# Attention with a mixture of experts: shared matmuls ahead of an output's first product, the normalisation over two steps, the router inside the projection, the slot table moved at other times

## The chip, the core and the metric

The kernel runs on one core of a Trainium2 chip. A core has TensorE (PE in the profile: matmuls; PEld: its weight loads), VectorE (DVE), ScalarE (ACT), GpSimd (POOL) and the DMA queues that SyncE (SP), ScalarE and GpSimd issue to. The metric is the device time of one execution in microseconds (us), as the median of several runs.

## The reference, cut to what matters

```python
x = L0_attn_x                                   # (2, 1024, 512)
xn = _layernorm(x)
x = x + _L0_attn_ref(xn, Wq, Wk, Wv, Wo) + _L0_ffn_ref(xn, router, bias, gate, up, down, shared ...)
# attention, 16 heads of 32
S = where(causal, Q K^T / sqrt(32), -1e30);  P = softmax(S);  out = (P V) @ Wo.T
# feed-forward, 2048 tokens
scores = sigmoid(x2d @ rw.T);  sfc = scores + bias            # 8 experts
# the best 2 of 4 groups of 2 experts, in them the best 2 experts, weights scaled to a sum of 2.5
routed = sum over e of cw[:, e] * ((silu(x2d @ gw[e].T) * (x2d @ uw[e].T)) @ dw[e].T)   # 352 wide
shared = (silu(x2d @ sg.T) * (x2d @ su.T)) @ sd.T                                       # 704 wide
out = routed + shared
```

## The kernel before

Each fp32 operand of the large products is split into a high and a low part, and three products stand for one (hi·hi, hi·lo, lo·hi). The program is five blocks, one after the other; a block begins when all engines have ended the one before.

1. `norm_phase`: normalises 16 tiles of 128 tokens, turns them into `xt_hi` and `xt_lo`, projects V. Its last steps split the router's weights into `r_hi` and `r_lo`.
2. `project_phase`: first the router, then Q and K. TensorE makes the router's logits for four blocks of 512 tokens (12 matmuls each into the one buffer `ps_r`, which ScalarE copies out in between), turns them, ScalarE takes the sigmoid, and GpSimd picks the experts. Then `multiply` makes 8 chunks of 128 rows of Q and K, four groups of 12 matmuls each; for each chunk ScalarE and VectorE split the weights (`split`, L524 and L654), and the results go out in two parts (`evacuate`). SP loads the weights of a chunk (L476), stores `xt` blocks and stores each chunk when it is evacuated, in one written order of steps.
3. `attend_phase`: 32 heads (16 for each of 2 batches) of 12 steps. Every engine runs the same loop over steps `s`, and a table of lags says what of which head it does in a step: at lag 0 the row maxima of scores (`maximum`, TensorE L1392 into one of two `ps_m`, VectorE L1272 or L1276 out of them), at lag 14 the maxima turned (`turn_row`, L1403) and sent through DRAM into a row of `qs` by ScalarE's queue (L1186, L1194), at 24 the scores (L1416), then exponential, the split into `prob_hi` and `prob_lo` (GpSimd L1160 in 10 of 12 steps, VectorE L1291 in 2), and at 30 the product with V (`value`, L1439 and L1441). A head has two outputs, one for each half of its queries; both build up in the one buffer `ps_o`. The first product of an output (`n in STARTS`) waits until ScalarE has copied the output before it (`o_copied`, L1218, in the same step's list). At lag 32 the copied output is turned into `ps_x`, and at 33 VectorE normalises it (`normalize`: L1307, L1308, L1310, L1315), before it takes that step's maximum. `turn_row` writes into the same bank `ps_x`, and so waits for `o_ready`, the end of L1315.
   In `shared(s)` TensorE puts 864 matmuls of the shared expert between the steps. A planner (`fill_counts`) deals them out by what each step costs TensorE. In the steps with the first product of an output it puts one to three.
   GpSimd makes the slot table of the routed tokens in between (`place`): it fills the table with pads, SP stores it to DRAM (L989, at `g == 1`), 32 indirect DMAs scatter the entries over it (L1130), and after the last step GpSimd reads it back (L1171) and waits for it.
4. `out_phase`: the attention's last product. 5. `routed_phase`: 39 tiles of gathered tokens.

## Time and profile before

| what | value |
|---|---|
| median of 3 runs | 1184.96 us (1183.19 to 1187.52) |
| profiled execution, its own time | 1182.23 us |
| its span | 1180.5 us |
| PE busy | 1064.8 us (90%), 5379 matmuls |
| DVE busy | 780.8 us (66%) |
| ACT busy | 647.6 us (55%) |
| POOL busy | 508.1 us (43%) |
| DMA moved | 165.70 MB, mean 140 GB/s |

The span is what the engines' records cover; the profiled execution's own time is 1.7 us longer. A matmul's recorded end is modelled, and matmuls overlap in the array: in an undisturbed run a matmul of 512 columns is recorded at 0.39 us while the next starts 0.23 us after it.
### The profile page before, as it was taken

Reading aid. Unit: us, or ns where it says so; the run is one execution under the profiler, and the core shown is the slowest. Engines: PE = TensorE matmul, PEld = TensorE weight load, DVE = VectorE, ACT = ScalarE, POOL = GpSimd, SP = SyncE. Lnnn points to the kernel's source line nnn. Section 1 sums busy time; section 2 is a strip of 40 time slices with the busy share of each in tenths; the row PEclk is TensorE's granted clock in tenths of the full one; section 3 lists DMA queues with packets and bytes.
Section 4 is the critical chain, followed back from the end, with each engine's and each line's share of the span. In section 5 each row is a group of like instructions: output and inputs, shape, how many; then the busy total and the mean of one; then the engine's idle time right before and its main releaser. Section 6 shows DMA issues by size and latency. Waiting matters only on the chain. (4 is left out here: it accounts for less than half of the span.)

```text
span 1180.5 us, 19294 instructions
## 1 busy us (share of the span) xinstructions
PE 1064.8 (90%) x5379; PEld 816.7 (69%) x5380; DVE 780.8 (66%) x1729; ACT 647.6 (55%) x1291; POOL 508.1 (43%) x567
## 2 busy tenths in 40 slices
PE   6979995888999999989999999978988999999994
PEld 4838883666677776767777777756766777777773
DVE  6822324556678868777777787645466777778772
ACT  4532220455777767777777777752154555555551
POOL 0008305289656555556556555651002333333331
PEclk9999995889899999999999999998989999999998
DMA  6969549978255264344345535018895443333342
GB/s 206 311 267 371 205 193 198 142 117 144 44 144 144 50 193 109 121 124 127 94 116 144 144 78 183 2 37 276 259 342 140 72 71 63 68 70 69 71 72 36
DMA packets 104648, 165.70 MB, mean 140 GB/s; under 512 B 49040, under 2 KB 59600, under 8 KB 101360
## 3 DMA queue, kind: packets, MB, share of 16 engines
q1 hardware_dynamic: 94128, 143.88, 42.8%
q0 software_dynamic: 9856, 20.53, 9.8%
q8 instruction: 38, 0.62, 0.2%
q14 instruction: 50, 0.41, 0.1%
q10 hardware_dynamic: 576, 0.26, 0.1%
HBM read 103.35 MB, written 61.28 MB: 139 GB/s over the span
## 5 line engine op out<-in xcount | busy, mean ns | idle before, releaser
L1160 POOL TENSOR_TENSOR prob_lo<-prob,prob_hi 128x512 fp32r<-128x512 f32 (+2 forms) x320 | 308.8, 978 | 239.6 <-ACT prob_hi L1209 223.9
L1202 ACT ACTIVATE prob<-ps_s 128x512 f32<-128x512 f32 (+3 forms) x384 | 188.2, 490 | 150.2 <-PE ps_s L1421 104.0
L1209 ACT ACTIVATE prob_hi<-prob 128x512 fp32r<-128x512 f32 (+3 forms) x384 | 198.5, 517 | 12.8 <-ACT row_stage L1183 12.7
L1272 DVE CUSTOM_DVE_ANT_0 ps_m<-ps_m,causal 128x384 f32<-128x384 f32 (+3 forms) x256 | 126.0, 498 | 69.8 <-PE ps_m L1392 68.9
L1828 DVE TENSOR_TENSOR rw_lo<-gu_sb,rw_hi 128x704 fp32r<-128x704 f32 x156 | 138.8, 893 | 47.9 <-ACT rw_hi L1763 42.2
L1742 POOL DMA_INDIRECT out<-work,rows x39 | 61.7, 1582 | 243.4 <-DVE rows L1789 118.0
L1392 PE MATMUL ps_m<-ks,qs 96*128 96x512 f32 (+3 forms) x384 | 143.7, 376 | 22.6 <-DMA ks<-qk_hi 13.6
L1439 PE MATMUL ps_o<-prob_hi,vs 128*66 128x512 f32 (+3 forms) x384 | 133.9, 349 | 18.8 <-issue 11.5
L1763 ACT ACTIVATE rw_hi<-gu_sb 128x704 fp32r x156 | 123.3, 792 | 46.6 <-PE ps_ru L1861 31.6
L1416 PE MATMUL ps_s<-qs,ks 97*128 97x512 f32 (+3 forms) x384 | 138.7, 361 | 2.4 <-ACT prob L1202 2.3
L1441 PE MATMUL ps_o<-prob_lo,vs 128*66 128x512 f32 (+3 forms) x384 | 131.1, 342 | 0.0
L1276 DVE TENSOR_REDUCE maxima<-ps_m 128x1 f32<-128x512 f32 x128 | 85.5, 685 | 65.7 <-PE ps_m L1392 65.4
L1392 PEld LDWEIGHTS ps_m<-ks,qs 96*128 96x128 f32 x384 | 75.4, 197 | 54.9 <-DVE maxima L1276 23.8
L1882 PE MATMUL ps_ry<-d_sb,work 128*128 (+1 forms) x234 | 106.9, 592 | 1.2 <-issue 1.2
L1416 PEld LDWEIGHTS ps_s<-qs,ks 97*128 97x128 f32 x384 | 74.2, 193 | 20.4 <-ACT prob L1202 4.7
L1439 PEld LDWEIGHTS ps_o<-prob_hi,vs 128*66 128x66 f32 x384 | 53.7, 140 | 43.5 <-issue 22.5
L1472 PE MATMUL ps_f<-xt,sg_hi 128*128 128x512 f32 (+1 forms) x192 | 74.7, 424 | 8.0 <-DVE gated L1325 4.3
L1754 ACT ACTIVATE xg_hi<-ps_xt 128x512 fp32r<-128x512 f32 x39 | 23.3, 598 | 85.9 <-PE ps_xt L1849 85.9
L1472 PE MATMUL ps_f<-xt,su_hi 128*128 128x512 f32 (+1 forms) x192 | 70.4, 400 | 0.0
L1882 PEld LDWEIGHTS ps_ry<-d_sb,work 128*128 128x128 f32 (+1 forms) x234 | 43.2, 190 | 38.8 <-issue 38.8
L662 DVE TENSOR_TENSOR work<-ps_q,work 128x512 fp32r<-128x512 f32 x32 | 22.2, 692 | 61.1 <-ACT work L531 61.1
L1421 PE MATMUL ps_s<-late,eye 128*128 128x128 f32 x256 | 61.2, 239 | 0.0
(212 smaller groups left out, 2422.4 us busy)
## 6 DMA issues: line engine op xcount, KB each, us to landing
xt<-xt_blocks SPq DMA_DIRECT2D x8, 2048.0 KB, 9.2
v_rows<-work SPq DMA_DIRECT2D x16, 512.0 KB, 2.9
qk_hi<-work SPq DMA_DIRECT2D x8, 1024.0 KB, 4.5
qk_lo<-work SPq DMA_DIRECT2D x8, 1024.0 KB, 7.1
qs<-qk_hi SPq DMA_DIRECT2D x64, 128.0 KB, 2.9
ks<-qk_hi SPq DMA_DIRECT2D x64, 128.0 KB, 3.1
vs<-v_rows SPq DMA_DIRECT2D x32, 256.0 KB, 4.8
out<-y_acc SPq DMA_DIRECT2D x32, 256.0 KB, 3.5
```

Source lines behind the costliest of these rows:

```text
L1160: nc.gpsimd.tensor_tensor(prob_lo[:, s % NPL, 0:w], prob[:, s % NP, 0:w], prob_hi[:, s % NPH, 0:w].bitcast(F32), ALU.subtract).then_inc(lo ...
L1202: nc.scalar.activation(prob[:, s % NP, 0:w], ps_s[s % NS][:, 0:w], ACT.Exp, scale=SCALE).then_inc(exp_done, 1)
L1209: nc.scalar.activation(prob_hi[:, s % NPH, 0:w], prob[:, s % NP, 0:w], ACT.Copy).then_inc(hi_ready, 1)
L1272: nc.vector.tensor_tensor_reduce(ps_m[s % NM][:, 0:w], ps_m[s % NM][:, 0:w], causal[:, TBW - w:], 1.0, MASKED, ALU.add, ALU.max, maxima[:, ...
L1392: nc.tensor.matmul(ps_m[s % NM][:, 0:w], qs[0:ROWS, c, t * P:(t + 1) * P], ks[0:ROWS, c, k0:k0 + w], start=True, stop=True).then_inc(m_don ...
L1416: last = nc.tensor.matmul(ps_s[s % NS][:, 0:w], ks[0:ROWS + 1, c, kt * P:(kt + 1) * P], qs[0:ROWS + 1, c, q0:q0 + w], start=True, stop=not ...
L1439: nc.tensor.matmul(into, vs[:, c, kt, :], prob_hi[:, s % NPH, 0:w], start=n in STARTS, stop=False)
L1441: nc.tensor.matmul(into, vs[:, c, kt, :], prob_lo[:, s % NPL, 0:w], start=False, stop=n in ENDS).then_inc(pv_done, 1)
L1472: last = nc.tensor.matmul(ps_f[part][0:w, :], (w_hi, w_lo, w_hi)[term][:, kc, f0:f0 + w], xt[:, (0, 0, 1)[term], kc, :], start=(j == 0), s ...
L1763: nc.scalar.activation(w_hi[:, k, :], chunk(e, k), ACT.Copy).then_inc(w_hi_ready, 1)
L1828: nc.vector.tensor_tensor(w_lo[:, k, :], chunk(e, k), w_hi[:, k, :].bitcast(F32), ALU.subtract).then_inc(w_lo_ready, 1)
L1882: last = nc.tensor.matmul(ps_y[c % 2][:, :], hid_t[0:w, c % HR, k, :], d_sb[0:w, bass.ds(e * NF + k, 1), :].rearrange("p a d -> p (a d)"), ...
```

## The change

- **TensorE in attention.** In a step with an output's first product, `shared(s)` now comes before `value`; in all others it stays behind it.
- **VectorE in attention.** `normalize` keeps the reciprocal and the copy; the sum and the multiplication become `weigh_o`, one step later and behind that step's maximum. Three semaphores become one.
- **Projection.** The router's four groups of 12 matmuls now each follow a group of the first chunk, and the turn follows the first group of the second chunk. The sigmoid comes after ScalarE's second copy of that chunk. The chunks' weights are converted first. ScalarE's wait for the stores of the norm block moves in front of its first copy-out.
- **Slot table.** Its pads are written by GpSimd at the start of the projection and stored by SP in step 5 of its list there, behind the load of chunk 5. The table is read back by SP in front of `load_values(15)`, at `g == 16`, and SP waits for it at the block's end.
- Some semaphores are merged, and ScalarE's loop over the chunks is unrolled.

```diff
@@ project_phase, SP
+                def store_pads(i, c):
+                    if i == 2 and c == 1:
+                        sp.wait_ge(table_padded, 3)
+                        sp.dma_start(slots_dram.rearrange("(j p) a -> p j a", p=P),
+                                     slot_table[:, :, :]).then_inc(pads_stored, 16)
-                pipeline(sp, CH, U, [(0, load), (0, store_xt), (1, load_shared), (2, store)],
+                pipeline(sp, CH, U, [(0, load), (0, store_xt), (1, load_shared), (0, store_pads), (2, store)],
                          back=CH)
+                sp.wait_ge(pads_stored, 16)
@@ ACT
+                        if t == 0:
+                            copy_logits(n)
+                        if t == 1 and n == 1:
+                            act.wait_ge(logits_turned, 1)
+                            nc.scalar.activation(score[:, :, :], ps_s[:, :, :],
+                                                 ACT.Sigmoid).then_inc(score_ready, 1)
-                pipeline(act, CH, U, [(0, split), (1, evacuate)])
+                pipeline(act, CH, U, [(0, split), (1, evacuate)], back=CH)
@@ PE
                         last.then_inc(q_done, 1)
+                        if t == 0:
+                            logits(n)
+                        if t == 1 and n == 0:
+                            turn_logits()
@@ attend_phase, SP
-                    if g == 1:
-                        sp.wait_ge(table_padded, 1)
-                        sp.dma_start(slots_dram.rearrange("(j p) a -> p j a", p=P),
-                                     slot_table[:, :, :]).then_inc(pads_stored, 16)
+                    if g == HEADS // 2:
+                        sp.wait_ge(entries_stored, 16 * 2 * NT)
+                        sp.dma_start(slot_table[:, :, :],
+                                     slots_dram.rearrange("(j p) a -> p j a", p=P)
+                                     ).then_inc(table_loaded, 16)
@@ GpSimd
-                pool.wait_ge(entries_stored, 16 * 2 * NT)
-                pool.dma_start(slot_table[:, :, :], slots_dram.rearrange("(j p) a -> p j a", p=P)
-                               ).then_inc(table_loaded, 16)
-                pool.wait_ge(table_loaded, 16)
@@ DVE
                     nc.vector.reciprocal(o_inv[:, :, :], ps_ot[:, :, 2 * DK:2 * DK + 1]).then_inc(normalizing, 1)
                     nc.vector.tensor_copy(o_part[:, :, :], ps_ot[:, :, DK:2 * DK]).then_inc(normalizing, 1)
+                def weigh_o(s):
...
+                    dve.wait_ge(normalizing, 3 * o + 2)
                     nc.vector.tensor_tensor(o_sum[:, :, :], ps_ot[:, :, 0:DK], o_part[:, :, :],
+                                            ALU.add).then_inc(normalizing, 1)
+                    dve.wait_ge(normalizing, 3 * o + 3)
...
-                    for lag, stage in ((NORM, normalize), (0, maximum), (LO, lo)):
+                    for lag, stage in ((NORM, normalize), (0, maximum), (LO, lo),
+                                       (NORM + 1, weigh_o)):
@@ PE
-                    for lag, stage in ((AHEAD, score), (VALUE, value)):
-                        if 0 <= s - lag < STEPS:
-                            stage(s - lag)
-                    shared(s)
+                    if 0 <= s - AHEAD < STEPS:
+                        score(s - AHEAD)
+                    starts = (s - VALUE) % NB in STARTS
+                    if starts:
+                        shared(s)
+                    if 0 <= s - VALUE < STEPS:
+                        value(s - VALUE)
+                    if not starts:
+                        shared(s)
```

TensorE in attention, from the maximum in front of a head's last block of the second output to the maximum of the next step. `ps_m` holds maxima, `ps_s` scores, `ps_o` the output, `ps_f` the shared expert. Before:

```order
L1392 MATMUL ps_m<-ks,qs 128x384
L1416 MATMUL ps_s<-qs,ks 128x512
L1439 MATMUL ps_o<-prob_hi,vs 66x512
L1441 MATMUL ps_o<-prob_lo,vs 66x512
L1497 MATMUL ps_f<-sd_lo,hid_hi 128x512
L1392 MATMUL ps_m<-ks,qs 128x512
```

The same place of TensorE's order now:

```order
L1409 MATMUL ps_m<-ks,qs 128x384
L1433 MATMUL ps_s<-qs,ks 128x512
L1514 MATMUL ps_f<-sd_lo,hid_hi 128x512
L1456 MATMUL ps_o<-prob_hi,vs 66x512
L1458 MATMUL ps_o<-prob_lo,vs 66x512
L1409 MATMUL ps_m<-ks,qs 128x512
```

One matmul of the shared expert (L1497, now L1514) has moved from behind the two products to between the score and the first product.

VectorE in attention, over the first two steps of a head, from the last maximum of the head before. Before:

```order
L1280 TENSOR_TENSOR maxima<-maxima 128x4
L1307 RECIPROCAL o_inv<-ps_x 128x4
L1308 COPY o_part<-ps_x 128x128
L1310 TENSOR_TENSOR o_sum<-ps_x,o_part 128x128
L1315 TENSOR_TENSOR work<-o_sum,o_inv 128x4x32
L1276 TENSOR_REDUCE maxima<-ps_m 128x1
L1352 TENSOR_TENSOR y_acc<-ps_f,y_acc 128x512
L1276 TENSOR_REDUCE maxima<-ps_m 128x1
```

VectorE's same place now:

```order
L1291 TENSOR_TENSOR maxima<-maxima 128x4
L1316 RECIPROCAL o_inv<-ps_x 128x4
L1317 COPY o_part<-ps_x 128x128
L1287 TENSOR_REDUCE maxima<-ps_m 128x1
L1368 TENSOR_TENSOR y_acc<-ps_f,y_acc 128x512
L1287 TENSOR_REDUCE maxima<-ps_m 128x1
L1327 TENSOR_TENSOR o_sum<-ps_x,o_part 128x128
L1331 TENSOR_TENSOR work<-o_sum,o_inv 128x4x32
```

The sum and the multiplication have moved behind two reductions (and, in this head, a sum of the shared expert); the first reduction now stands right behind the copy.

SP's queue in attention at `g == 16`, now:

```order
L960 DMA ks<-qk_hi 32x1024
L1010 DMA slot_table<-slots 128x39x2
L967 DMA vs<-v_rows 128x8x64
L998 DMA gu_raw<-in_sgate 128x4x96
L998 DMA gu_raw<-in_sup 128x4x96
```

The table's read stands between the rows of head 16 and the values of head 15; before, GpSimd issued it after its last step.

## Rows read from the trace of the kernel before

**Rows 1.** Busy time by stretch: span, us (x instructions) of each engine, PEclk, DMA, GB/s.
```profile
69.40:88.40 19.00, 14.47 (x64) 5.33 (x64) 0.72 (x2) 4.94 (x8) 1.61 (x4) 0.91 0.72 272
88.40:176.90 88.50, 88.42 (x416) 72.88 (x416) 27.78 (x46) 21.68 (x38) 35.76 (x62) 1.00 0.68 256
...
305.00:755.00 450.00, 430.09 (x2361) 330.37 (x2360) 352.81 (x909) 334.83 (x758) 253.03 (x264) 1.00 0.42 119
```

**Rows 2.** Timeline of the projection's start: start us, us, engine, line, [idle before <-releaser].
```profile
69.49 0.43 PE L543 MATMUL ps_r<-xt_hi,r_hi 128*8 128x512 f32 x1 [2.52 <-PEq L228]
...
69.83 0.46 SPq L476 DMA_DIRECT2D w_raw<-in_wqk  x1
...
87.03 1.14 ACT L524 ACTIVATE w_hi<-w_raw 128x512 fp32r<-128x512 f32 x2
...
88.42 0.50 PE L563 MATMUL ps_q<-xt_hi,w_hi 128*128 128x512 f32 x1 [1.68 <-DVE w_lo L654]
```

**Rows 3.** Landing of the eight loads of the chunks' weights (`w_raw`).
```profile
DMA to landing us min/median/max: 3.2/7.0/8.1
```

**Rows 4.** A stretch while the pads are stored, columns as in rows 1.
```profile
200.00:204.00 4.00, 4.00 (x14) 3.11 (x13) 1.46 (x3) 0.00 (x0) 0.04 (x1) 0.65 2.08 2
```

**Rows 5.** DMA issues: queue, count, KB each, median us to landing.
```profile
slots<-slot_table SPq DMA_DIRECT2D x1, 39.0 KB, 27.6
slot_table<-slots POOLq DMA_DIRECT2D x1, 39.0 KB, 6.6
```

**Rows 6.** Timeline of attention's first head, behind the pads' store.
```profile
216.44 0.60 ACT L1226 ACTIVATE tanh<-ps_f 128x512 f32<-128x512 f32 x1 [6.67 <-DMA max_rows<-row_stage]
...
217.81 0.74 PE L1472 MATMUL ps_f<-xt,sg_hi 128*96 128x512 f32 x1 [4.31 <-DVE gated L1325]
...
221.87 0.79 PE L1416 MATMUL ps_s<-qs,ks 97*128 97x512 f32 x1
```

**Rows 7.** An output's first product: timeline, and its group from 305 to 755 us.
```profile
561.88 0.39 PE L1416 MATMUL ps_s<-qs,ks 97*128 97x512 f32 x1
562.45 0.41 PE L1439 MATMUL ps_o<-prob_hi,vs 128*66 128x512 f32 x1 [0.18 <-issue]
...
L1439 PE MATMUL ps_o<-prob_hi,vs 128*66 128x512 f32 (+3 forms) x317 | 109.3, 345 | 10.9 <-issue 6.3 <-ACT o_copy L1218 4.6
```

**Rows 8.** Normalisation and maxima: timeline, group (305 to 755 us), lines' minimum/median/maximum ns.
```profile
572.15 0.29 DVE L1310 TENSOR_TENSOR o_sum<-ps_x,o_part 128x128 f32<-128x128 f32 x1
572.49 0.40 PE L1392 MATMUL ps_m<-ks,qs 96*128 96x512 f32 x1
572.55 0.84 DVE L1315 TENSOR_TENSOR work<-o_sum,o_inv 128x128 f32<-128x128 f32 x1
573.32 0.68 DVE L1276 TENSOR_REDUCE maxima<-ps_m 128x1 f32<-128x512 f32 x1
574.05 0.44 PE L1392 MATMUL ps_m<-ks,qs 96*128 96x384 f32 x1 [0.23 <-DVE maxima L1276]
574.33 0.27 PE L1403 MATMUL ps_x<-ident,maxima 128*8 128x128 f32 x1
...
L1392 PE MATMUL ps_m<-ks,qs 96*128 96x512 f32 (+3 forms) x316 | 114.0, 361 | 6.0 <-DVE maxima L1276 5.0
...
L1315 DVE TENSOR_TENSOR work<-o_sum,o_inv x64: 292/712/1921, 241.4 to 791.3; 128x128 f32<-128x128 f32 x64
...
L1280 DVE TENSOR_TENSOR maxima<-maxima x32: 164/910/1101, 198.5 to 754.6; 128x4 f32<-128x4 f32 x32
```

**Rows 9.** Timeline of attention's end.
```profile
788.56 2.10 POOL L1171 DMA_DIRECT2D slot_table<-slots  x1
...
798.37 0.34 DVE L1603 COPY rows<-slot_table 128x1 int32<-128x1 int32 x4 [6.76 <-PEq L923]
```

**Rows 10.** ScalarE's queue in a middle head: the row of maxima stored, then loaded.
```profile
471.37 0.27 ACTq L1186 DMA_DIRECT2D max_rows<-row_stage  x1
477.98 0.22 ACTq L1194 DMA_DIRECT2D qs<-max_rows  x1
```

More of the change, by code:

```diff
@@ L429, in project_phase @@
         bias_b = sbuf("bias_b", [P, 1, E])
+        pads = sbuf("pads", [P, 1], I32)
         score = sbuf("score", [P, NT, E])
@@ L501, in store_xt, with copy_logits @@
                                      ).then_inc(xt_stored, 16)
-                pipeline(sp, CH, U, [(0, load), (0, store_xt), (1, load_shared), (2, store)],
+                pipeline(sp, CH, U, [(0, load), (0, store_xt), (1, load_shared), (0, store_pads), (2, store)],
                          back=CH)
                 sp.wait_ge(xt_stored, 32 * NTB)
+                sp.wait_ge(pads_stored, 16)
             @block.scalar
             def _(act):
-                act.wait_ge(zeros_stored, 32)
-                for slot_stored in norm_stored:
-                    act.wait_ge(slot_stored, 16 * (NT // NORM_SLOTS))
-                for n in range(NTB):
+                def copy_logits(n):
                     act.wait_ge(logits_done, n + 1)
@@ L516, in _ @@
                                          ACT.Copy).then_inc(logits_copied, 1)
-                act.wait_ge(logits_turned, 1)
-                nc.scalar.activation(score[:, :, :], ps_s[:, :, :], ACT.Sigmoid).then_inc(score_ready, 1)
                 def split(i, c):
@@ L527, in evacuate @@
                     t = U * i + c
+                    if t == 0:
+                        act.wait_ge(zeros_stored, 32)
+                        for slot_stored in norm_stored:
+                            act.wait_ge(slot_stored, 16 * (NT // NORM_SLOTS))
                     wait(act, stored[c], 32 * i)
@@ L532, in evacuate, with logits @@
                                              ACT.Copy).then_inc(q_hi_ready, 1)
-                pipeline(act, CH, U, [(0, split), (1, evacuate)])
+                        if t == 0:
[5 more added lines that the diff above has]
+                pipeline(act, CH, U, [(0, split), (1, evacuate)], back=CH)
             @block.tensor
             def _(pe):
-                for n in range(NTB):
-                    pe.wait_ge(logits_copied, n) if n else None
+                def logits(n):
+                    wait(pe, logits_copied, n)
                     j = 0
@@ L547, in _, with turn_logits @@
                     last.then_inc(logits_done, 1)
-                pe.wait_ge(logits_copied, NTB)
-                for t in range(NT):
-                    last = nc.tensor.transpose(ps_s[:, t, :], logits_t[:, t * P:(t + 1) * P],
-                                               ident[0:E, 0:E])
-                last.then_inc(logits_turned, 1)
+                def turn_logits():
+                    pe.wait_ge(logits_copied, NTB)
+                    for t in range(NT):
+                        last = nc.tensor.transpose(ps_s[:, t, :], logits_t[:, t * P:(t + 1) * P],
+                                                   ident[0:E, 0:E])
+                    last.then_inc(logits_turned, 1)
                 def multiply(i, c):
@@ L588, in _ @@
             def _(pool):
+                nc.gpsimd.iota(pads[:, :], pattern=[[0, 1]], base=T, channel_multiplier=1
+                               ).then_inc(table_padded, 1)
+                nc.gpsimd.memset(slot_table[:, :, 1], 0.0).then_inc(table_padded, 1)
+                pool.wait_ge(table_padded, 2)
+                nc.gpsimd.tensor_copy(slot_table[:, :, 0].bitcast(I32),
+                                      pads[:, :].broadcast_to([P, NST])).then_inc(table_padded, 1)
                 nc.gpsimd.memset(ones[:, :], 1.0).then_inc(ones_ready, 1)
@@ L658, in evacuate @@
                     t = U * i + c
+                    if t == U - 1:
+                        dve.wait_ge(logits_turned, 1)
                     for n in range(NTB):
@@ L847, in attend_phase @@
         tile_no = sbuf("tile_no", [P, NST, 1])
-        pads = sbuf("pads", [P, 1], I32)
         tokens = sbuf("tokens", [P, NT], I32)
@@ L1033, in place @@
                 def place():
-                    then(nc.gpsimd.iota(pads[:, :], pattern=[[0, 1]], base=T, channel_multiplier=1))
-                    then(nc.gpsimd.memset(slot_table[:, :, 1], 0.0))
-                    yield
-                    placed()
-                    nc.gpsimd.tensor_copy(slot_table[:, :, 0].bitcast(I32),
-                                          pads[:, :].broadcast_to([P, NST])).then_inc(table_padded, 1)
-                    yield
                     then(nc.gpsimd.iota(tokens[:, :], pattern=[[P, NT]], base=0,
@@ L1298, in normalize @@
                     half = BLOCKS[s % NB][0]
-                    g = s // NB
-                    h, b = g // B, g % B
-                    o = 2 * g + half
+                    o = 2 * (s // NB) + half
                     dve.wait_ge(o_turned, o + 1)
```

65 lines of the change are left out of this document (31 added, 34 removed).

## The prediction

> **What bounds the kernel now.** I read three views. The busy time by stretch comes first [rows 1]: in the projection TensorE is busy 88.42 of 88.50 us at full clock, and in the body of attention 430 of 450 us, while no other engine comes near. So in both a term counts only if it shortens what TensorE does or waits for. Then the timelines at the seams of the blocks: the projection begins with router work in which TensorE is busy 14.47 of 19.00 us [rows 1, 2], attention's first head stands on a row of maxima [rows 6], and its end on GpSimd's table read [rows 9]. Last the groups and timelines inside a head, for the two places at which TensorE waits in the body: an output's first product [rows 7] and the third maximum of a head [rows 8]. The page's engine shares alone would have hidden both, since matmuls overlap in the record: between starts at 561.88 and 562.45 lie 0.57 us where 0.23 would do, so 0.34 are lost, of which the record calls 0.18 idle [rows 7].
>
> **Part 1, shared matmuls in front.** A stretch of 27 heads has 54 first products. The group's idle time is 10.9 us [rows 7]; if each also hides the 0.16 us by which an end is recorded late (0.34 less 0.18), the loss is at most 10.9 + 54 x 0.16 = 19.5 us, 0.20 to 0.36 us for each. What is put in front costs 0.23 us each, and it is work that TensorE does anyway, one to three of them, so most of such a wait is covered. Over 64 outputs the waits are 13 to 23 us. I take 15 saved. The far ends: 20 saved; and 3 lost, if the covered waits are replaced (a moved matmul waits for its own input, or a product that did not wait comes one or two matmuls later and ScalarE's chain after it).
>
> **Part 2, the normalisation over two steps.** What goes: in the head shown, the third maximum starts at 574.05 after 0.23 us recorded idle plus the 0.16, so 0.39 lost, because the reduction that frees its buffer starts only at 573.32, behind the multiplication [rows 8]. The group's idle, 6.0 us over 27 heads, plus 0.16 for each, is the same 0.38. Now that reduction comes right behind the copy, and the wait goes. What comes: turning the maxima waits for the multiplication's end. That now stands behind the second maximum (start 572.49) and its reduction: 0.40 for the matmul, 0.68 for the reduction, 0.29 for the sum, 0.11 up to the multiplication (572.15 + 0.29 to 572.55) and 0.71 for itself, the line's median: 2.19 us after 572.49. TensorE's own work reaches the turn 574.33 - 572.49 - 0.39 = 1.45 us after it. So it waits 0.74, less the 0.39 gone: 0.35 us a head, and a little more for the semaphores between. Behind the waiting turn on TensorE stand the next scores and products, so all of it counts: 31 heads x 0.39 = 12 us more. The ends: at the line's shortest, 0.29, it comes to 31 x (0.35 - 0.42) = -2 us; at 1.10, the longest of a similar instruction (L1280), 31 x (0.35 + 0.39) = +23. The second output's normalisation is in a step where nothing waits for it: nothing.
>
> How long the multiplication takes is the disputed number: 292 ns at best, 712 in the median [rows 8], for the same shape. The Trainium skill has a rule for it (SBUF — State Buffer, "Who interferes with whom"): a VectorE instruction with two SBUF inputs and a GpSimd instruction that reads SBUF exclude each other for a whole instruction. L1310, which has one input in PSUM, takes 0.29 in the same head, and L1315, with both in SBUF, 0.84: the rows agree. By that rule the multiplication goes on waiting wherever GpSimd is at work, and the term stays near +12; without it, it would be near -2.
>
> **Part 3, the pads' store leaves attention.** Around it DMA stands: from 200 to 204 us 2 GB/s are moved at a share of 2.08 [rows 4], and the store of 39 KB lands after 27.6 us [rows 5]. ScalarE cannot load the row of maxima and stands 6.67 us, so `gated` is late, and TensorE stands 4.31 us until 217.81 [rows 6]. Its matmuls behind that pause are recorded at 0.74 and 0.79 us instead of 0.39 [rows 6], so the 221.87 - 217.81 = 4.1 us to the first score would be about 2. So 4.3 + 2 = 6.3, and the rest of the slow stretch and the late rows of the next head, which I put at 1.7: 8 us saved (5 to 11). What is late next is the row itself, in its normal 6.6 us [rows 10], which five steps cover.
>
> **Part 4, the table's read leaves the end.** GpSimd issues it at 788.56 and it lands 6.6 us later [rows 5, 9]; VectorE stands 6.76 us until 798.37, so it had ended at 791.61. Without the read the next block follows VectorE's end by the seam alone. At the projection's start TensorE's whole pause, seam and all that it waited for, was 2.52 us [rows 2], so the seam is between nothing and that: the block begins at 791.6 to 794.1, which is 6.8 to 4.3 us earlier. I take 5.5.
>
> **Part 5, the read in the middle.** The same 39 KB, now in pieces through SP's queue beside head 16's rows. Nothing of it is needed there; what it can delay is the row of maxima, stored at 471.37 and loaded at 477.98 [rows 10], with about five steps of room in front and four behind it. A step is 450 / 324 = 1.39 us, so the room is 12.5 us. If the read takes 6.6 us it is hidden; if it takes the pads' 27.6, ScalarE stands and TensorE with it, up to 27.6 - 12.5 = 15 us. The nearer row is the read's own, 6.6, so I take +1.5. The Trainium skill speaks against a gain from the change of queue (DMA: Bandwidth & Descriptors, "Issuing engines are not separate DMA queues"): all issuers share the same 16 engines, and the rows of ScalarE's queue interleave with SP's. No run here shows this for a read of the table.
>
> **Part 6, the projection.** No matmul goes. The router work, 14.47 us with its slow-clock part (the stretch's mean clock is 0.91 [rows 1]), no longer waits for ScalarE's copies, but TensorE now begins only when the first weights are there: issued at 69.83, landed 3.2 to 8.1 us later [rows 2, 3], 4 if nothing is in front of it, and then 88.42 - 87.03 = 1.39 for both conversions: 75.2. Plus 14.47 it is 89.7 where the chunks' work stood alone at 88.42: 1.3 us later, and the pause before is longer, so more of it may be at half clock. I take +1.5 (0 to 5). The sigmoid, and with it GpSimd's routing, comes 17 to 20 us later; GpSimd is busy 35.76 of the 88.50 us, so it has that room. The pads' store is hidden if the weights behind it come in time: chunk 6's are issued a chunk (88.5 / 8 = 11 us) after it and used two chunks later (about 21). At worst 27.6 - 11 + 8.1 - 21 = 3.7 us late. In the median nothing.
>
> **The sum.** -15 + 12 - 8 - 5.5 + 1.5 + 1.5 = -13.5 us, against the profiled execution's 1182.2: 1168.7. That execution was 2.7 us under the median 1184.96; on the median it is 1171.5, and I say 1172.
>
> **Rivals.**
> A, the multiplication finds GpSimd idle. Where it stands now, a step later, GpSimd waits for ScalarE more often; then part 2 is -2 and the sum -27.5: 1157.5. For it: the range down to 292 ns; GpSimd is busy only 253 of 450 us [rows 1]. Against: the median.
> B, the transfers' cost moves instead of going. The pads delay the projection's weights (+3.7), and the table's read costs ScalarE and TensorE 8 in the middle, half of its far end: -13.5 + 3.7 + 6.5 = -3.3: 1181.7. Against it: DMA's mean share in the body is 0.42 [rows 1].
> C, the order of the shared matmuls gives nothing, since ScalarE's chain sets when the next scores and products can go: -13.5 + 15 = +1.5: 1186.5. Against it: ScalarE is busy 335 of 450 us.
> D, slower: the turn of the maxima takes more than all the rest gives. Without part 2 the sum is -25.5, so it is slower from (25.5 + 3.6) / 31 = 0.94 us a head, with a multiplication of 0.94 - 0.39 + 0.71 = 1.26 us. If each took the 1.92 of the line's longest, a head would lose 0.39 + 1.21 = 1.60, in all 49.6: +24, 1209. In heads with a sum of the shared expert between the two reductions 0.68 comes on top. Against: L1280, caught in the same way, is at most 1.10.
>
> **How the numbers follow.** A measurement of this kernel tells a change from none at about 0.3%, 3.6 us. Forecast 0.50, A 0.18, B 0.09, C 0.11, D 0.12 (its milder cases mostly, 1189 to 1200). Faster: 0.48 of the forecast's 0.50 + 0.18 of A + 0.04 of B, and 0.02 of C = 0.72. Within: 0.02 + 0.05 + 0.07 = 0.14. Slower: 0.12 of D and 0.02 of C = 0.14. The likeliest case alone, from its own ends: 1162 to 1181. The range, to leave out 2 in 10: 1156 to 1187.
>
> **What would show it.** First products: the group's idle time of PE falls from 10.9 to under 3 us in the same stretch. Part 2: L1392 no longer waits for VectorE, and the turn of the maxima starts late behind the second half of the normalisation, by some 0.7 us; if that line's median is near 0.3, A holds. Part 3: ScalarE's wait of 6.67 us for `max_rows` and TensorE's of 4.31 are gone, and the first score comes at full clock. Part 4: out_phase begins within 3 us of VectorE's last instruction. Part 5: ScalarE shows no wait for `max_rows` near head 16. Part 6: the projection's last matmul ends 0 to 3 us later than 176.9. The forecast is wrong if the body of attention does not get shorter by 2 to 5 us, or if the seams together give under 8.

## The result and the profile after

The changed kernel takes 1166.35 us (median of 4 runs, 1161.82 to 1170.92), the kernel before beside it 1184.08: a ratio of 0.985, 95% interval 0.980 to 0.989. It is faster, as forecast, by 17.7 us where about 13 were forecast (1172 against a median of 1184.96). The profiled execution took 1170.92, span 1169.1, and is the slowest of the four; against the 1182.23 of the profiled execution of before the difference is only 11.3 (13.5 forecast). One of the six executions of e9 below ran in a slower state (1216.45 us at a granted clock of 0.83), so the time given there is the median of the other five (over all six it is 1154.11).

Busy time by stretch of the changed kernel, to hold against [rows 1]; the columns are those of the view there:

```profile
69.40:88.40 19.00, 11.94 (x42) 7.77 (x43) 2.92 (x6) 3.04 (x5) 0.86 (x5) 0.73 0.91 345
88.40:176.90 88.50, 87.38 (x423) 68.99 (x421) 27.68 (x43) 22.85 (x39) 35.88 (x63) 1.00 0.91 240
305.00:755.00 450.00, 428.23 (x2407) 335.52 (x2406) 343.39 (x912) 341.45 (x775) 257.98 (x270) 1.00 0.43 119
```

TensorE is still what bounds both blocks.

Where the time went between the two profiled executions is read from the starts of TensorE's maxima (12 a head) and of the first and last instructions of each block. In the changed kernel's timeline head 6 starts in the first of these rows and head 30 in the second, 402.1 us later:

```profile
308.99 0.40 PE L1409 MATMUL ps_m<-ks,qs 96*128 96x512 f32 x1
711.09 0.40 PE L1409 MATMUL ps_m<-ks,qs 96*128 96x512 f32 x1
```

Taken in this way for every kernel that was run (us; the first trace of the changed kernel, and a second one, e0):

```
stretch                               before  changed    e0
norm's last matmul to projection's     109.8    112.6  111.9
projection's last to first maximum      12.8     12.9   12.6
first maximum to head 2                 35.1     27.1   26.1
head 2 to head 6                        86.4     88.0   87.0
head 6 to head 30                      410.4    402.1  401.7
head 30 to last product of attention    67.8     66.8   66.8
last product to first expert's gate     74.9     70.2   68.3
first to last expert's gate            294.6    299.5  295.8
```

The two traces of one and the same kernel differ by 10.4 us in their spans, of which 0.4 lie in heads 6 to 30; 3.7 lie in the experts. So the totals of single traces say little about a term of a few us, while the stretch of heads 6 to 30 tells 1 us (in five traces of kernels that are the same there it is 401.7 to 402.1). In what follows a part's price is taken from its own stretch, and the timed ratio stands beside it.

The rows that answer to those shown ahead. The projection's start [rows 2]:

```profile
71.22 0.46 SPq L476 DMA_DIRECT2D w_raw<-in_wqk  x1
75.05 0.63 ACT L526 ACTIVATE w_hi<-w_raw 128x512 fp32r<-128x512 f32 x1 [5.94 <-DMA w_raw<-in_wqk]
76.46 0.79 PE L577 MATMUL ps_q<-xt_hi,w_hi 128*128 128x512 f32 x1 [8.10 <-DVE w_lo L679]
77.05 0.63 PE L577 MATMUL ps_q<-xt_hi,w_lo 128*128 128x512 f32 x1
81.65 0.40 PE L555 MATMUL ps_r<-xt_hi,r_hi 128*8 128x512 f32 x1
```

TensorE stands 8.10 us until the first weights are there and converted, where it stood 2.52. Its matmuls are 0.63 long up to 81.3, at the granted clock of 0.5 (1.2 GHz). The trace has that clock from 71.3 to 81.5, 10.2 us, but it fell within the pause; in the columns of [rows 1]:

```profile
71.40:76.40 5.00, 0.00 (x0) 0.00 (x0) 0.69 (x1) 0.63 (x1) 0.48 (x3) 0.50 0.75 264
76.50:81.40 4.90, 4.90 (x12) 3.84 (x13) 0.00 (x0) 0.54 (x1) 0.00 (x0) 0.50 1.05 408
```

So TensorE works at half clock for 5.1 us, which costs it 2.5; in the kernel before it was 3.4 us (69.7 to 73.1), all of it with TensorE at work, which cost 1.7.

The first row of maxima [rows 6], issued, landed and used:

```profile
208.93 0.55 ACTq L1197 DMA_DIRECT2D max_rows<-row_stage  x1
213.76 0.22 ACTq L1205 DMA_DIRECT2D qs<-max_rows  x1
214.88 0.60 ACT L1237 ACTIVATE tanh<-ps_f 128x512 f32<-128x512 f32 x1 [0.49 <-PE ps_f L1489]
219.95 0.39 PE L1433 MATMUL ps_s<-qs,ks 97*128 97x512 f32 x1
```

It is read back 4.8 us after its store, no wait for `max_rows` is left (ScalarE's 6.67 us), and the first score runs at full clock (0.39).

Groups of instructions by line: 305 to 755 us for the first three [rows 7, 8]; the last is the turn of the maxima, from 305 to 740:

```profile
L1409 PE MATMUL ps_m<-ks,qs 96*128 96x512 f32 (+3 forms) x315 | 110.8, 352 | 0.0
L1456 PE MATMUL ps_o<-prob_hi,vs 128*66 128x512 f32 x323 | 109.9, 340 | 2.7 <-ACT o_copy L1229 1.8 <-issue 0.9
L1331 DVE TENSOR_TENSOR work<-o_sum,o_inv 128x128 f32<-128x128 f32 x54 | 26.0, 482 | 1.9
L1420 PE MATMUL ps_x<-ident,maxima 128*8 128x128 f32 x26 | 7.0, 269 | 18.3 <-DVE work L1331 18.3
```

The idle time in front of the value products fell from 10.9 to 2.7, that in front of the maxima from 6.0 to nothing; but the turn of the maxima (L1420), which had none before, now has 18.3 us, and all of it ends with the multiplication (`work`, L1331). The timeline of one head shows how:

```profile
563.10 0.68 DVE L1287 TENSOR_REDUCE maxima<-ps_m 128x1 f32<-128x512 f32 x1
563.70 0.28 DVE L1327 TENSOR_TENSOR o_sum<-ps_x,o_part 128x128 f32<-128x128 f32 x1
564.01 0.48 DVE L1331 TENSOR_TENSOR work<-o_sum,o_inv 128x128 f32<-128x128 f32 x1
564.64 0.27 PE L1420 MATMUL ps_x<-ident,maxima 128*8 128x128 f32 x1 [0.78 <-DVE work L1331]
```

The turn starts 0.15 us after the multiplication's end, and so it does in the median of 27 heads. It needs nothing that the multiplication writes. It writes a bank of PSUM, `ps_x`, which the outputs' products share, and the last instruction that reads that bank is the sum at 563.70.

The end of attention [rows 9], and the read in the middle that replaces it, with the row of maxima beside it [rows 10]:

```profile
461.03 0.42 SPq L1010 DMA_DIRECT2D slot_table<-slots  x1
464.58 0.27 ACTq L1197 DMA_DIRECT2D max_rows<-row_stage  x1
470.96 0.22 ACTq L1205 DMA_DIRECT2D qs<-max_rows  x1
779.76 0.29 DVE L1331 TENSOR_TENSOR work<-o_sum,o_inv 128x128 f32<-128x128 f32 x1
780.37 0.34 DVE L1626 COPY rows<-slot_table 128x1 int32<-128x1 int32 x4 [0.32 <-PEq L944]
```

VectorE's pause there is 0.32 us instead of 6.76. The table's transfers by issue, with their time to landing at the end of the row [rows 5]:

```profile
slots<-slot_table SPq DMA_DIRECT2D x1, 39.0 KB, 23.3
slot_table<-slots SPq DMA_DIRECT2D x1, 39.0 KB, 5.6
```

### The profile page after: what moved, and what is told of

Its sections match the earlier page's. It is cut to its first block and busy times, and to the rows that moved or that the text cites. A ratio compares the mean times of both kernels' runs of the same rounds, so it can differ in the third digit from the quotient of the medians.

```text
span 1169.1 us, 19196 instructions
## 1 busy us (share of the span) xinstructions
PE 1055.6 (90%) x5379; PEld 819.2 (70%) x5380; DVE 769.1 (66%) x1729; ACT 647.0 (55%) x1291; POOL 505.2 (43%) x566
## 5 line engine op out<-in xcount | busy, mean ns | idle before, releaser
L1283 DVE CUSTOM_DVE_ANT_0 ps_m<-ps_m,causal 128x384 f32<-128x384 f32 (+3 forms) x256 | 126.8, 496 | 75.2 <-PE ps_m L1409 74.1
L1409 PE MATMUL ps_m<-ks,qs 96*128 96x512 f32 (+3 forms) x384 | 140.0, 366 | 13.8 <-DMA ks<-qk_hi 12.8
L1456 PEld LDWEIGHTS ps_o<-prob_hi,vs 128*66 128x66 f32 x384 | 53.6, 140 | 29.2 <-issue 13.8
L1777 ACT ACTIVATE xg_hi<-ps_xt 128x512 fp32r<-128x512 f32 x39 | 23.3, 598 | 91.3 <-PE ps_xt L1872 91.3
```

The lines of the kernel that those rows point to most:

```text
L1283: nc.vector.tensor_tensor_reduce(ps_m[s % NM][:, 0:w], ps_m[s % NM][:, 0:w], causal[:, TBW - w:], 1.0, MASKED, ALU.add, ALU.max, maxima[:, ...
L1409: nc.tensor.matmul(ps_m[s % NM][:, 0:w], qs[0:ROWS, c, t * P:(t + 1) * P], ks[0:ROWS, c, k0:k0 + w], start=True, stop=True).then_inc(m_don ...
L1456: nc.tensor.matmul(into, vs[:, c, kt, :], prob_hi[:, s % NPH, 0:w], start=n in STARTS, stop=False)
```

## The experiments

All ratios are to the kernel before, timed on the same chip in the same rounds; the changed kernel itself stood at 0.985 (0.980 to 0.989) and in e0 at 0.983 (0.979 to 0.987). "Heads 6 to 30" is the stretch of the table above.

**e0, the changed kernel again.** No edit.

> The changed kernel once more, unchanged, as the measure for the others. Its first traced execution spent 4.9 us more than the kernel before between the first and the last gate product of the routed experts (299.5 against 294.6), code that the change does not touch. Theory S: that is scatter of single executions; a second trace shows 294 to 297 there and the median stays at 1166 +- 2. Rival G: the transfers of the experts' weights start earlier beside other traffic and give part of the gain back; then 298 to 301 again.

Measured: 1162.35 us; 295.8 us between the experts' gates, where the first trace had 299.5. In the traces of the kernels below it was 293.0 to 298.9, without order, 296.4 in the mean. The kernel before had 294.6 in its one trace, and e11, which has the kernel before's code there, had 298.1. So the 4.9 us are within the scatter of single traces, and a loss in the experts is not shown. The median came out 4 us under the first one's, more than I had allowed.

**e1, part 1 undone.**

```
-                    if starts:
-                        shared(s)
                     if 0 <= s - VALUE < STEPS:
                         value(s - VALUE)
-                    if not starts:
-                        shared(s)
+                    shared(s)
```

> Changed kernel with part 1 undone: the shared matmuls stand behind the value products in every step. Theory of part 1 (they cover the wait of an output's first product): the first products' starts are late again by some 10 us each way in steps 6 and 10 of a head over 26 heads (now 3.4 and 2.8, in the kernel before 10.0 and 8.7), and the time is 10 to 15 us longer: 1176 to 1181. Rival C (the order gives nothing, ScalarE's chain sets the pace): 1164 to 1169.

Measured: 1177.57 us, ratio 0.994 (0.992 to 0.997), 15.2 us above e0, which was timed beside it; heads 6 to 30 take 414.1, 12.1 more than the changed kernel. The group of the value products, 305 to 740 us:

```profile
L1456 PE MATMUL ps_o<-prob_hi,vs 128*66 128x512 f32 (+3 forms) x303 | 104.1, 343 | 10.3 <-issue 5.6 <-ACT o_copy L1229 4.6
```

The idle time is back, and with the same releasers as in [rows 7]. 12.1 us over 24 heads are 0.50 a head, 16 over 32. Rival C is out.

**e2, part 2 undone.** The sum and the multiplication stand in `normalize` again, ahead of the maximum.

```
-                def weigh_o(s):
-                    if s % NB not in ENDS:
-                        return
...
-                    for lag, stage in ((NORM, normalize), (0, maximum), (LO, lo),
-                                       (NORM + 1, weigh_o)):
+                    for lag, stage in ((NORM, normalize), (0, maximum), (LO, lo)):
```

> Changed kernel with part 2 undone: reciprocal, copy, sum and multiplication in one step, ahead of the maximum. Theory of part 2 (it costs, since the turn of the maxima waits 0.77 us more a head, and only 0.38 are given back at the third maximum): 31 x 0.39 = 12 us shorter, 1154. Rival A (splitting gains or is neutral): 1165 to 1169.

Measured: 1157.52 us, ratio 0.978 (0.975 to 0.982), an interval that overlaps e0's; heads 6 to 30 take 395.0, 7.1 less. Groups of maxima and of their turn, 305 to 740 us:

```profile
L1402 PE MATMUL ps_m<-ks,qs 96*128 96x512 f32 (+3 forms) x311 | 112.3, 361 | 6.0 <-DVE maxima L1287 5.0
L1413 PE MATMUL ps_x<-ident,maxima 128*8 128x128 f32 x27 | 7.4, 273 | 0.0
```

The one wait has gone and the other has come back: 18.3 us in front of the turn against 6.0 in front of the maxima. So splitting the normalisation, as it was done, costs time: 0.29 us a head. The timed difference to e0 is 4.8 us, less than the 7.1 of these 24 heads.

**e6, TensorE waits for the sum.** One edit in the changed kernel, in the two turns (the sum is the third of three counts in `normalizing`):

```
-                    wait(pe, o_ready, turned["outputs"])
+                    wait(pe, normalizing, 3 * turned["outputs"])
...
-                    wait(pe, o_ready, o)
+                    wait(pe, normalizing, 3 * o)
```

> Changed kernel with one edit: TensorE's turns wait for the sum and not for the multiplication; the order on VectorE is untouched. Theory (the turn of the maxima starts 0.15 us behind the multiplication's end in 26 of 27 heads, so it is that which it waits for): the wait of 0.88 us a head falls by the multiplication and its start, 0.6 to 0.75, 31 x 0.65 = 20 us shorter, 1146 (1142 to 1150). Rival W (another wait stands right behind it): under 8 us shorter, 1158 to 1166.

Measured: 1149.33 us, ratio 0.969 (0.967 to 0.972); heads 6 to 30 take 387.4, 14.7 less, which is 0.61 a head and 19 over 31 heads. The turn's group, 305 to 740 us:

```profile
L1420 PE MATMUL ps_x<-ident,maxima 128*8 128x128 f32 x27 | 7.3, 271 | 2.6 <-DVE o_sum L1327 2.5
```

The releaser is now the sum, and of 18.3 us 2.6 are left. This settles what the turn waited for: a semaphore that stood for more than was needed.

**e7, the sum first, the product last.** e6, and the sum back in `normalize`, with the multiplication behind the same step's maximum.

```
                     nc.vector.tensor_copy(o_part[:, :, :], ps_ot[:, :, DK:2 * DK]).then_inc(normalizing, 1)
+                    dve.wait_ge(normalizing, 3 * o + 2)
+                    nc.vector.tensor_tensor(o_sum[:, :, :], ps_ot[:, :, 0:DK], o_part[:, :, :],
+                                            ALU.add).then_inc(normalizing, 1)
...
-                                       (NORM + 1, weigh_o)):
+                                       (NORM, weigh_o)):
```

> Changed kernel with two edits in the normalisation: TensorE's turns of maxima and outputs wait for the sum, the last instruction that reads their PSUM bank, and no longer for the multiplication, which reads SBUF alone; and the sum goes back to the first step, with the multiplication behind that step's maximum. Theory: both waits go, the third maximum's and that of the turn (22.8 us over 26 heads in the changed kernel's trace, 0.88 each): 31 x 0.85 = 26 us shorter, 1140 (1136 to 1146). Rival W (the turn finds another wait, for ScalarE's read of the row or for the second reduction): under 10 us shorter, 1156 to 1164.

Measured: 1147.39 us, ratio 0.969 (0.966 to 0.972). Neither number was hit: 15 us below e0, with heads 6 to 30 at 385.6, so 16.5 saved there where 20 had been expected. The turn's wait went, but the multiplication, 0.59 us long in the mean, now stands in front of the fourth maximum's reduction: over 26 heads TensorE's starts are 1.2 us later there than in e6, 0.8 at the fifth score, and a little more among the shared matmuls. e6 had already taken nearly all that was to be had.

**e9, the product reads PSUM.**

```
-                    nc.vector.tensor_tensor(o_sum[:, :, :], ps_ot[:, :, 0:DK], o_part[:, :, :],
+                    nc.vector.tensor_tensor(ps_ot[:, :, 0:DK], ps_ot[:, :, 0:DK], o_part[:, :, :],
...
-                    nc.vector.tensor_tensor(attended[:, tiles, h * DK:(h + 1) * DK], o_sum[:, :, :],
+                    nc.vector.tensor_tensor(attended[:, tiles, h * DK:(h + 1) * DK], ps_ot[:, :, 0:DK],
```

> Changed kernel with one edit: the sum is written back into its PSUM bank and the multiplication reads it there, so that it has one input in SBUF and not two; order and waits are untouched. So far the multiplication of a head's first half takes 0.68 us in the mean beside GpSimd, and that of the second half 0.29 in each of the 28 heads in which GpSimd stands idle. Theory (two SBUF inputs wait for a GpSimd instruction that reads SBUF): the first half's falls to about 0.3, the wait of the turn from 0.88 to 0.5 us a head, and heads 6 to 30 take 9 to 10 us less than 402: 392.5; in all 12 us shorter, 1150 to 1152. Rival (what stretches it is its output or its broadcast operand, both still in SBUF): it stays at 0.6 to 0.7, and heads 6 to 30 at 401 to 403.

Measured: 1152.77 us, ratio 0.973 (0.970 to 0.976); heads 6 to 30 take 393.3. The multiplication's group from 305 to 755 us, and the turn's from 305 to 740:

```profile
L1331 DVE TENSOR_TENSOR work<-ps_x,o_inv 128x128 f32<-128x128 f32 x55 | 16.0, 292 | 1.9
L1420 PE MATMUL ps_x<-ident,maxima 128*8 128x128 f32 x27 | 7.3, 270 | 8.7 <-DVE work L1331 8.1
```

Its mean is 292 ns where the changed kernel had 482, and 0.29 us is also its longest, although GpSimd is at work during each of the 28 of a first half. The output and the broadcast operand are where they were, so it is the second input in SBUF that made it wait. With 8.8 us less for 24 heads the forecast of 9 to 10 was met within 1 us.

**e10, the product a step later.** e7 with `(NORM + 1, weigh_o)`, as the change had it.

> Changed kernel with the sum in the first step, TensorE's turns waiting for the sum, and the multiplication where the change put it, a step later. In the kernel with the product behind the same step's maximum, heads 6 to 30 took 385.6 us, with 1.2 us more of waits at the fourth maximum of a head and 0.8 at the scores than in the others. Theory (the product in that step makes the next reduction late): these go, 383.5 to 384.5 for heads 6 to 30, and the whole is 1 to 2 us shorter than that kernel: 1145 to 1147. Rival: the sum ahead of the reduction costs them, so nothing changes or it gets 1 us longer: 385.5 to 387.

Measured: 1145.72 us, ratio 0.967 (0.964 to 0.970); heads 6 to 30 take 383.1, a little under what was expected. Maxima and their turn, 305 to 740 us:

```profile
L1409 PE MATMUL ps_m<-ks,qs 96*128 96x512 f32 (+3 forms) x315 | 111.6, 354 | 0.0
L1420 PE MATMUL ps_x<-ident,maxima 128*8 128x128 f32 x27 | 7.4, 273 | 0.0
```

Both waits are gone. This version beats both kernels: by its ratio it takes 3.3% off the kernel before, against 1.5 to 1.7% for the change.

**e11, part 1 alone in the kernel before.** The reverse of e1's diff.

> The kernel before with part 1 alone: the shared matmuls stand in front of an output's first product. Heads 6 to 30 took 410.4 us in the kernel before, of which 1.7 are a stretch at half clock. Theory (part 1 is worth the same 0.50 us a head alone as in the changed kernel, where undoing it cost 12.1 us over these 24 heads): 396 to 398.5 for heads 6 to 30, the whole 16 us shorter than before, 1169. Rival (the parts overlap: with the one-step normalisation the covered wait shows elsewhere): 400 to 404, and 1173 to 1178.

Measured: 1173.67 us, ratio 0.991 (0.989 to 0.993), 10.5 us under its neighbour where 16 were expected; heads 6 to 30 take 396.6, 13.8 less than before, or 12.1 without the 1.7 us that a half-clock stretch cost the trace of before. So in its own stretch the part is worth the same 0.50 us a head alone or with the others. From e11 to the changed kernel, which adds part 2 and the parts that act elsewhere, the stretch grows by 5.5 us, 0.23 a head, where e2 says 7.1. Why the timed gain is smaller than the 16 us that follow from that is not settled: its 11 runs spread over 15 us, and its traced execution had a span of 1163.8, 16.7 under that of before.

**e3, part 3 undone.** The pads are stored from attention's loop over heads again.

```
-                pipeline(sp, CH, U, [(0, load), (0, store_xt), (1, load_shared), (0, store_pads), (2, store)],
+                pipeline(sp, CH, U, [(0, load), (0, store_xt), (1, load_shared), (2, store)],
...
+                    if g == 1:
+                        sp.dma_start(slots_dram.rearrange("(j p) a -> p j a", p=P),
+                                     slot_table[:, :, :]).then_inc(pads_stored, 16)
```

> Changed kernel with part 3 undone: the pads of the slot table are stored in the attention block beside its second head's loads, where the kernel before had them. Theory of part 3 (the small pieces of that store hold up the first heads' rows of maxima and with them ScalarE and TensorE): from attention's first maximum to head 2 the time goes from 27.1 back to 35 us, the whole 6 to 9 us longer than the changed kernel, 1172 to 1175. Rival: the projection had hidden nothing, its block gets shorter by 3 to 4 us, and the net is 3 to 5: 1169 to 1171.

Measured: 1172.51 us, ratio 0.990 (0.987 to 0.992); first maximum to head 2 34.7 us, and the projection's block 111.1, where the kernels with the store in it have 112.5 in the mean (under e4). e11, which has the store in attention too, takes 32.5 from the first maximum to head 2. The row of maxima in this kernel:

```profile
205.73 0.57 ACTq L1194 DMA_DIRECT2D max_rows<-row_stage  x1
218.55 0.22 ACTq L1202 DMA_DIRECT2D qs<-max_rows  x1
218.88 0.60 ACT L1234 ACTIVATE tanh<-ps_f 128x512 f32<-128x512 f32 x1 [7.69 <-DMA max_rows<-row_stage]
220.25 0.74 PE L1486 MATMUL ps_f<-xt,sg_hi 128*96 128x512 f32 x1 [5.31 <-DVE gated L1338]
```

12.8 us from store to load instead of 4.8, and ScalarE's and TensorE's waits of [rows 6] are back.

**e5, parts 4 and 5 undone.**

```
-                    if g == HEADS // 2:
-                        sp.wait_ge(entries_stored, 16 * 2 * NT)
-                        sp.dma_start(slot_table[:, :, :],
...
+                pool.wait_ge(entries_stored, 16 * 2 * NT)
+                pool.dma_start(slot_table[:, :, :], slots_dram.rearrange("(j p) a -> p j a", p=P)
+                               ).then_inc(table_loaded, 16)
+                pool.wait_ge(table_loaded, 16)
```

> Changed kernel with parts 4 and 5 undone: GpSimd reads the slot table at the end of attention. Theory: VectorE stands 6.8 us again between its last multiplication and the next block's first copy (0.32 in the changed kernel), and nothing else changes: 6.4 us longer, 1173. Rival: the next block is bound by its transfers (its share of DMA time is 0.75 to 0.87), which don't start earlier than their buffers allow; then what the earlier start brings is mostly lost behind it and the kernel is 1 to 3 us longer, 1167 to 1169.

Measured: 1169.84 us, ratio 0.986 (0.984 to 0.989): between the two theories in the total, and by its interval not told from the changed kernel. The trace decides: the read is issued at 776.82, and VectorE's first copy comes after 7.24 us.

```profile
776.82 2.10 POOL L1180 DMA_DIRECT2D slot_table<-slots  x1
779.51 0.29 DVE L1329 TENSOR_TENSOR work<-o_sum,o_inv 128x128 f32<-128x128 f32 x1
787.04 0.34 DVE L1624 COPY rows<-slot_table 128x1 int32<-128x1 int32 x4 [7.24 <-PEq L944]
```

From the last product to the first expert's gate it takes 76.6 us, the kernel before 74.9 and e11, which has the read at the end as well, 74.1; all the others have it in the middle and take 66.2 to 70.9. So the 6.4 us are kept behind the seam, as far as single traces can tell that differ by up to 4.7 among themselves. Heads 6 to 30 take 402.0 without the read in them and 402.1 with it.

**e4, part 6 undone.** Logits in front of the projection (`pipeline(pe, ...)`), as in the kernel before.

> Changed kernel with part 6 undone: the logits' matmuls stand in front of the projection, as before. In the changed kernel's trace TensorE starts the projection 8.1 us after the block before it (2.5 in the kernel before) and then has 10.2 us at half clock (3.4), and the whole projection takes 2.8 us longer; attention from head 2 to head 6 takes 1.6 us longer. Theory P (both are the router's new place): 3 to 4.5 us shorter than the changed kernel, 1162 to 1163.5. Rival: they are scatter or have other causes (pads, routing), within 1.5 us of it.

Measured: 1163.83 us, ratio 0.982 (0.979 to 0.985): nothing that can be told from e0 or from the changed kernel's 0.985, so theory P is not borne out. The projection's block takes 112.5 us, with a second stretch of 3.4 us at half clock in it, at 89.77; without the 1.7 us that this costs it is 110.8. Counted in the same way, the nine traces with the router inside and the pads' store in the projection (changed, e0, e1, e2, e5, e6, e7, e9, e10) have 111.3 to 113.7, 112.5 in the mean. With e12, the kernel before and e11 (111.2, or 109.5 without a second stretch of 3.4 us at half clock, at 88.70) the two causes come apart:

```
projection's block, us            pads' store elsewhere   pads' store in it
router in front of the projection      109.8, 109.5          110.8, 111.8
router inside it                       111.1                 112.5 (nine traces)
```

The router's place makes it 1.2 to 1.5 us longer and the pads' store 1.4 to 1.7; with a scatter of 2.4 us between traces of one kind, neither is known to better than about 1. And head 2 to head 6 takes 87.7, where the changed kernel's two traces have 88.0 and 87.0: the 1.6 us there had nothing to do with the router.

**e12, e10 with the router in front.**

> The kernel of the product a step later, with the router's matmuls back in front of the projection. Theory: nothing to tell from that kernel, within 2 us: heads 6 to 30 the same within 0.5 us, and the projection's block within 1.5 us of 111.5 once a half-clock stretch in it is taken off. Rival: the router in front is worth the 2.5 us by which the pause of TensorE at the projection's start is longer in the changed kernel; then 2 to 4 us shorter.

Measured: 1144.60 us, ratio 0.967 (0.964 to 0.970); heads 6 to 30 at 383.4, the projection's block at 111.8. The same as e10, as expected.

## Why the prediction was right, and where it was not

The direction holds, and the mechanism of each part. By the steps:

*Part 1, -15.* Right, in sum and mechanism: -16 by the stretch in e1 and in e11, inside the ends of -20 and +3; timed, e1 is 15.2 us above e0 and e11 10.5 below its neighbour. What carried it was reading the loss from the starts of the matmuls; the idle times alone give 10.9 us over 27 heads. The check of under 3 us of idle time holds (2.7).

*Part 2, +12.* The mechanism was right, the size too large by a third or more. By the starts of TensorE's matmuls the turn's loss rose from 0.12 to 0.88 us a head, 0.76 where 0.74 were worked out, and the third maximum's fell from 0.42 to 0.01, 0.41 where 0.39 were. That makes +0.35; heads 6 to 30 say 0.29 by e2, +9 over 31 heads, and 0.23 by e11, +7. What remains is spread over the shared matmuls, whose lost time also falls. The 12 had come from rounding 0.35 up to 0.39 for semaphores, and that addition was the part that was not there. That the 0.71 taken for the multiplication came so near was partly luck: it was the median over both halves of a head, whose means were 0.69 and 0.87 in the kernel before, and only the first half's counts (0.67 now).

One check was badly chosen. I had said that a median near 0.3 of the multiplication's line would speak for rival A. The median is 0.32, and A is wrong all the same: the 27 multiplications of the first halves take 0.67 in the mean, beside GpSimd, and it is these that the turn waits for; the 27 of the second halves found GpSimd idle and take 0.29 each (0.87 before), which nothing waits for. A line's median over two populations was no evidence for either.

The rule that was weighed there holds. The Trainium skill (SBUF — State Buffer, "Who interferes with whom") says that a VectorE instruction with two SBUF inputs contends with a GpSimd instruction that reads SBUF. The runs agree: by e9 the same multiplication with one of its inputs in PSUM takes 0.29 us beside a working GpSimd, every time, where it took 0.67 in the mean.

*Part 3, -8.* Right: first maximum to head 2 went from 35.1 to 27.1 and 26.1, and back to 34.7 in e3; e11, with the store in attention, has 32.5, so by single traces the part is worth 5.4 to 9 us, inside its ends of 5 and 11.

*Part 4, -5.5.* 6.4 (6.76 less 0.32), inside the ends. Of the seam that I had left between nothing and 2.52 us there is 0.32. I had taken TensorE's whole pause at the projection's start as its upper end; 1.45 us of that pause passed before VectorE's last instruction of the block before had ended (`r_lo`, in the trace of before: 68.24 + 0.18 us), so the seam was at most 1.07 us even there.

*Part 5, +1.5.* Nothing, 402.0 against 402.1. The read landed in 5.6 us, and the row beside it was loaded 6.4 us after its store, in [rows 10] 6.6. The Trainium skill's rule (DMA: Bandwidth & Descriptors, "Issuing engines are not separate DMA queues"), by which the queues share 16 engines, did not bear on this read: no delay is to be seen here. With the pads it did, and this case shows it: a store in SP's queue held up a row in ScalarE's, 12.8 us from store to load in e3 instead of 4.8.

*Part 6, +1.5.* Right in size: 1.2, from 112.5 us for the block in the mean of nine traces to 111.3 in the two with the router in front (e4 without its extra stretch at half clock, e12); and 1.3 to 1.6 without the pads' store (e3 against the kernel before and e11). The scatter leaves it known to about 1 us. The first step of the working was right: TensorE begins at 76.46 where 75.2 was forecast, and the block before ended 1.4 later in this trace. From that block's last matmul it is 5.6 us later than in the kernel before, and the half clock costs 2.5 us instead of 1.7. What pays for most of these 6.4 us is that TensorE no longer stands for ScalarE's copies of the logits and for the first weights. In the kernel before:

```profile
74.75 0.41 PE L543 MATMUL ps_r<-xt_hi,r_hi 128*8 128x512 f32 x1 [0.76 <-ACT work L515]
78.36 0.41 PE L543 MATMUL ps_r<-xt_hi,r_hi 128*8 128x512 f32 x1 [0.68 <-ACT work L515]
81.98 0.41 PE L543 MATMUL ps_r<-xt_hi,r_hi 128*8 128x512 f32 x1 [0.68 <-ACT work L515]
85.59 1.15 PE L550 MATMUL ps_s<-ident,work 8*128 8x8 f32 x16 [0.68 <-ACT work L515]
```

With the 1.68 us in front of the first chunk [rows 2] these are 4.5 us, and 5.3 with 0.16 us for each late-recorded end: 6.4 less 5.3 is 1.1.

The pads' store, which I had put at nothing, costs the block another 1.4 (112.5 against e3's 111.1). So the projection's last matmul ended 4.1 us after 176.9 in the first trace, outside the 0 to 3 of my check, and 2.0 in the second.

*The sum.* With the measured terms it is -16 + 9 - 8 - 6.4 + 0 + 1.2 + 1.4 = -18.8, between the 17.7 and, by e0's ratio, 20 of the timed medians. The terms come from single stretches, so that the sum meets the total this closely is in part luck: over heads 6 to 30 parts 1 and 2, by e1 and e2, make 5.0 us of the 6.6 that were measured. The forecast was 5 us short of it: 3 from part 2, 1 to 1.5 each from parts 1, 4 and 5, less the 1.4 of the pads. Of these part 2 was the term most mis-sized, 12 where 7 to 9 were measured. My last check, that the body of attention gets shorter by 2 to 5 us, was missed, though on the good side: 6.6 us for heads 6 to 30, once the clock's 1.7 are taken off.

*The rivals.* B: the read in the middle cost nothing where B had 8, the pads some 1.4 us where it had 3.7. C fell by e1. D had the right place, the turn of the maxima, and the wrong price: 0.29 us a head, where 0.94 were needed. A would have needed 0.3 us for the first halves' multiplications.

## What to carry to other kernels

Ask of a wait what the waiting instruction really needs. Here a matmul waited for an operation's last instruction, though the last reader of the shared PSUM bank was the one before it. Moving these two behind a reduction turned a wait of 6 us into one of 18. Letting the matmul wait for the last reader took 15 us off 24 heads' 402, and 19 with the sum ahead of the reduction again. To price a part of a few us, compare the stretch of the timeline in which it acts over many repeats: spans of the same kernel differed by 10 us, the 24 heads by 0.4. And where an instruction has two kinds of neighbours, take its durations apart before using the median.

## What the hardware showed

- A 128x128 multiplication on VectorE took 0.29 us with one input in PSUM, beside a working GpSimd (e9), and 0.34 to 0.87 us (mean 0.67) with both in SBUF (the changed kernel's first halves); with GpSimd idle it took 0.29 in either place.
- The store of 39 KB in small pieces landed after 23.3 us in the projection and cost its block some 1.4 us; in attention the same store delayed a row of maxima by 8 us.
- TensorE stood from 68.4 to 76.5 at the projection's start; the granted clock fell to 0.5 at 71.3 and was back at 1 at 81.5, so that TensorE worked at half clock for 5.1 us, which cost 2.5. After the pause of 2.5 us in the kernel before it worked so for 3.4 us, which cost 1.7. Within full work a single stretch of 3.4 us at 0.5 came in some executions and not in others (at 157.97 in e1, 424.70 in the kernel before), each worth 1.7 us; no cause of it is to be seen.
